# TensorE issues the score matmuls of four row strips one behind another in the pass for the exponentials

## What is computed

```python
qkv = x @ w_qkv                                    # x: 4096 tokens as 32 blocks of 128
scores = einsum('bhqd,bhkd->bhqk', q, k) / sqrt(8) # per sequence of 256 tokens, 16 heads
scores = where(causal, scores, finfo.min)
attn = softmax(scores, -1)
o = einsum('bhqk,bhkd->bhqd', attn, v) ... @ w_o
h = layernorm(x + o, g1, b1)
# then a mixture of 8 experts, 2 chosen per token, F = 512, and a second layernorm
```

## Time and profile before

| | us |
|---|---|
| median of 3 runs | 1197.24 |
| lowest and highest | 1195.87 and 1200.68 |
| profiled execution, first to last instruction (span) | 1192.8 |
| PE busy in it | 1022.4 (86%) |
| PE weight loads | 818.6 (69%) |
| DVE, ACT, POOL busy | 680.8, 670.5, 572.7 |

### The profile page before, as it was taken

How to read it: one execution, slowest core, us unless ns; L and a number is a source line. 1 busy time by engine, 2 the same in 40 slices (tenths; PEclk the granted TensorE clock), 3 DMA queues, 4 the chain that set the end, 5 groups by cost and what they waited for, 6 DMA issues and landing times. The chain is left out here.

```text
span 1192.8 us, 29724 instructions
## 1 busy us (share of the span) xinstructions
PE 1022.4 (86%) x10913; PEld 818.6 (69%) x10913; DVE 680.8 (57%) x2458; ACT 670.5 (56%) x1494; POOL 572.7 (48%) x693
## 2 busy tenths in 40 slices
PE   4799979998989989999989989998999988866470
PEld 2566656886877867686777867687777866766470
DVE  5657665655558835686568835686556723520314
ACT  1243424875758756675667757576666756534240
POOL 2223356235465455555565455554464456542515
PEclk9988877998999989898999979799999979887795
DMA  3394105555555545555556545555556545676562
GB/s 71 86 193 109 37 19 162 167 164 181 154 160 150 172 138 156 147 154 172 149 154 171 165 137 144 153 158 154 160 163 176 170 137 164 202 244 221 212 194 51
DMA packets 117239, 181.01 MB, mean 152 GB/s; under 512 B 13128, under 2 KB 80232, under 8 KB 117096
## 3 DMA queue, kind: packets, MB, share of 16 engines
q1 hardware_dynamic: 108904, 162.32, 47.7%
q0 software_dynamic: 8192, 16.79, 4.9%
HBM read 145.10 MB, written 38.68 MB: 154 GB/s over the span
## 5 line engine op out<-in xcount | busy, mean ns | idle before, releaser
L1173 POOL TENSOR_SCALAR_AFFINE_SELECT probs<-probs 128x512 f32<-128x512 f32 x256 | 182.5, 721 | 262.1 <-ACT probs L706 257.1
L706 ACT ACTIVATE probs<-ps_quad 128x768 f32<-128x768 f32 x256 | 193.7, 807 | 150.3 <-PE ps_quad L527 87.8
L744 ACT ACTIVATE act<-ps_ring,weights 128x128 f32<-128x128 f32 x696 | 191.8, 387 | 96.4 <-PE ps_ring L623 48.0
L874 DVE TENSOR_REDUCE shift_cols<-ps_quad 128x2 f32<-128x512 f32 (+3 forms) x256 | 149.9, 586 | 139.8 <-PE ps_quad L508 125.6
L632 PE MATMUL ps_ring<-weights,act 128*128 128x128 f32 x1392 | 190.8, 285 | 31.1 <-issue 16.4
L632 PEld LDWEIGHTS ps_ring<-weights,act 128*128 128x128 f32 x1392 | 174.5, 198 | 35.1 <-issue 21.6
L623 PE MATMUL ps_ring<-tile_t,weights 128*128 128x128 f32 x1392 | 187.6, 292 | 3.9 <-issue 3.2
L623 PEld LDWEIGHTS ps_ring<-tile_t,weights 128*128 128x128 f32 x1392 | 174.0, 204 | 16.8 <-issue 13.2
L1236 POOL DMA_INDIRECT picked<-sorted_outputs,place x128 | 123.7, 966 | 79.8 <-issue 78.6
L999 DVE TENSOR_TENSOR tile_y<-ps_ring,weights 128x128 f32<-128x128 f32 x174 | 48.8, 287 | 182.2 <-PE ps_ring L632 101.2
L1222 POOL DMA_INDIRECT sorted_rows<-h_rows,place x128 | 124.5, 972 | 53.5 <-issue 34.6
(11 more groups left out here) (165 smaller groups left out, 1531.5 us busy)
## 6 DMA issues: line engine op xcount, KB each, us to landing
weights<-expert_weights SPq DMA_DIRECT2D x174, 578.0 KB
tile_rows<-sorted_rows SPq DMA_DIRECT2D x56, 192.0 KB
sorted_outputs<-tile_y SPq DMA_DIRECT2D x56, 192.0 KB
query_key_parts<-qk SPq DMA_DIRECT2D x32, 256.0 KB, 5.0
k<-query_key_parts SPq DMA_DIRECT2D x64, 64.0 KB
q<-query_key_parts SPq DMA_DIRECT2D x64, 64.0 KB
sorted_rows<-zeros SPq DMA_DIRECT2D x2, 1472.0 KB, 10.7
xs<-in_L_attn_x SPq DMA_DIRECT2D x32, 64.0 KB, 2.3
```

Of the source, the lines that this page charges most:

```text
L706: sc.activation(probs[:, r % PROBS, 2 * a:2 * a + 2, :], ps_quad[:, 2 * a:2 * a + 2, 0:3 * P], ACT.Exp, scale=HD ** -0.5).then_inc(pair_fr ...
L744: ins = sc.activation(act[:, k % ACTS, f, :], bank(use)[:, f * P:(f + 1) * P], ACT.Gelu_apprx_tanh, bias=weights_of(k)[:, 2 * F + f:2 * F ...
L874: dve.tensor_reduce(shift_cols[:, late, groups], ps_quad[:, groups, 0:split], AX.X, ALU.max)
L1173: pool.affine_select(out=both, in_=both, compare_op=ALU.is_ge, fill=0.0, base=0, pattern=[[0, 2], [0, 2], [1, P]], channel_multiplier=-1). ...
```

## The change

In `exps` on PE the loop over pairs is split. PE first waits for both pairs to be free. Then it issues L523 for the strips 0 to 3, then L527 for the strips 0 to 3; `pair_full[0]` is signalled by the L527 of strip 1 and `pair_full[1]` by that of strip 3. Nothing else is changed: the same matmuls run on the same operands, `scores` stays as it was, and so do ACT, DVE, POOL and all DMAs. (Lines of PE behind `exps` move down by one.)

```diff
                 for a in range(2):
                     pe.wait_ge(pair_free[a], QUAD_NO["exps", n, j])
-                    for i in (2 * a, 2 * a + 1):
-                        rows = slice(32 * i, 32 * i + SLOT)
-                        pe.matmul(ps_quad[:, i, 0:P], k4[rows, par, j, at + P:at + S], q4s[rows, n % 2, j, P:S],
-                                  start=True, stop=True, tile_position=(32 * i, 0))
-                    for i in (2 * a, 2 * a + 1):
-                        rows = slice(32 * i, 32 * i + SLOT)
-                        mm = pe.matmul(ps_quad[:, i, P:3 * P], k4[rows, par, j, at:at + P], q4s[rows, n % 2, j, :],
-                                       start=True, stop=True, tile_position=(32 * i, 0))
-                    mm.then_inc(pair_full[a], 1)
+                for i in range(4):
+                    rows = slice(32 * i, 32 * i + SLOT)
+                    pe.matmul(ps_quad[:, i, 0:P], k4[rows, par, j, at + P:at + S], q4s[rows, n % 2, j, P:S],
+                              start=True, stop=True, tile_position=(32 * i, 0))
+                for i in range(4):
+                    rows = slice(32 * i, 32 * i + SLOT)
+                    mm = pe.matmul(ps_quad[:, i, P:3 * P], k4[rows, par, j, at:at + P], q4s[rows, n % 2, j, :],
+                                   start=True, stop=True, tile_position=(32 * i, 0))
+                    if i % 2:
+                        mm.then_inc(pair_full[i // 2], 1)
```

## The result

The changed kernel takes 1231.22 us (median of 4 runs, 1222.29 to 1238.12), the kernel before 1198.44 us (4 runs, 1195.87 to 1200.68). The ratio is 1.0263, with an interval of 1.0203 to 1.0322: about 33 us slower. The forecast was 1206 us, and at most 1214.

A forecast was written before the change was run, and what follows sets the result against it. PE's in-order list, with its few waits, was taken to set the pace. Late pair 0 cost 12.9 us, other terms 0; 30% absorbed left +9.0 us on 1197.2, so 1206 us, range 1197 to 1214.

The forecast's parts named there:

- rival B: In `exps` on PE, pairs run one after the other, so packing four strips gains 30 us: 1168 us; chance 0.05.
- step 2: PE's exit from waiting `exps` pieces: still 0.85 us after pair 1 is free, so cost 0.
- step 7: PE's other waits, such as "issue", absorb 30% of the 12.9 us delay, leaving +9.0 us.
- L: Theory formed after the result: the loss comes from ACT getting pair 0 of `exps` late, costing more than 9 us.
- step 4: Late pair 0 delays PE's next `scores` in 31 of 70 waiting pieces, 12.9 us; 39 pieces hide it.
- Step 1: Matmuls and loads of `exps`: none added or removed, cost 0, bounds -2 to +3 us.
- The check in the prediction: Sign to look for: PE's time from the last start to the exit of `exps` stays 0.85 to 0.88 us.
- Steps 3 and 4: ACT gets pair 0 of `exps` late, up to 0.73 us; PE feels it in 31 pieces, 12.9 us together.
- Step 6: ACT's copies and GELUs queued behind `exps` run late: 0 to 5 us, taken as 0.
- Rival A: PE's "issue" waits absorb 60 to 90% of the delay, no change: 1198 to 1202 us; chance 0.26.
- W: Theory formed after the result: waiting for both pairs has its own price on PE, paid in each waiting `exps` piece.

The follow-up runs named there:

- E4: Kernel before plus one wait, always already met, ahead of pair 1's own wait in `exps`; order and signals as before: 1209.88 us, ratio 1.0088.
- E3: Kernel before, PE's order and waits untouched, but pair 0 is signalled to ACT only by pair 1's matmuls: 1219.6 us, ratio 1.0164.
- E2: Kernel before with both waits ahead of the matmuls in `exps`, which still run pair by pair: 1227.01 us, ratio 1.0230.
- E1: Changed kernel with its two waits in the other order, pair 1's first: 1223.56 us, ratio 1.0190 to the kernel before.
- E9: Kernel before with pair 0's signal late only in the 31 `exps` pieces the prediction charged: 1069.06 us, ratio 1.0166.
- E10: Kernel before with pair 0's signal late only in the 39 `exps` pieces the prediction called hidden: 1054.92 us, ratio 1.0018.
- E5: The changed kernel once more, as it is, on another chip: 1221.59 us, ratio 1.0300 to the kernel before.
- E8: Kernel before with pair 0's mask matmuls L508, in the maxima pass, moved ahead of pair 1: 1190.08 us, ratio 1.0051.
- E6: Kernel before with the change, waits swapped, only in 58 `exps` pieces picked as having free banks: 1194.02 us, ratio 1.0072.
- E12: Kernel before with both waits ahead in the 58 pieces picked as free, matmuls still pair by pair: 1058.08 us, ratio 1.0057.

## Why the prediction was wrong

The direction was right, and so was the first reading: four strips are in flight already, there is nothing to pack (rival B), and what the change does is to hold pair 0 back. The size was wrong by a factor of over three and a half, 9 us for 33, and the steps that failed can be named. Of the 24 us that the forecast missed, step 2 is some 10 (E4), step 7 is 3.9, and L is 7 us larger than the 12.9 of step 4 (E3).

- **Step 1** (matmuls and loads cost nothing) holds. The order of the strips costs nothing that shows: E2 without it is as slow as the change. A free piece has its next load 0.881 us after its first before and 0.868 us after, at the median, within this step's bounds.
- **Step 2 failed.** It took PE's time from "pair 1 is free" to the exit as the same, 0.85 us, and the price of waiting as nothing. It is 0.06 us more to the first load and 0.04 us more to the exit, 0.105 us in each of some 70 pieces. Of the 43 ns at the exit some 13 come from pair 0 running beside pair 1 (E1's exit is 867 ns, for 854 before) and 30 from the wait that stands alone. Together that is 7.4 us; E4 measures 0.9%, 10 us, for the wait alone. The section on the change has the row that shows it: `[waits pair_free1,pair_free0]` on one matmul, where each had one wait before. The check in the prediction ("0.85 to 0.88 us") caught it: the exit is 0.897.
- **Steps 3 and 4 hold in place and are somewhat small.** E9 and E10 split the 70 pieces where step 4 does, and the one costs 1.7%, the other 0.2% with zero inside its interval. The steps of 0.67 and 0.22 us are measured as 0.675 and 0.23. The sum was 12.9; it is 14.4 between those two runs, and 17 us (12.6 to 22.2) for E9 against the kernel before. On the first chip, with the 39 other pieces late too, E3 gives 20 us (15 to 24). Where the 7 us above 12.9 arise isn't shown.
- **Step 6** (other work of ACT, 0 to 5 us) is E10's 0.2%, 2 us with an interval from -1.6 to +5.4. Taking 0 was fair.
- **Step 7 failed.** It let PE's waits for "issue" take up 30% of the delay, with 9.0 us left. They took up none that shows: the late signals cost at least 14.9 us in E3 and 12.6 in E9 by their intervals. In the rows of PE's matmuls, "issue" adds up to 44.7 us in 69 places before and 55.4 us in 79 after, and to 55 and 56.9 us in E3 and E4; these waits rather grow with the delay, though that is one trace of each. On the third chip, where such waits nearly vanish, L costs as much (E9, 1.7%). Rival A is out.
- **The granted clock**, which no step had, may make up some of the rest. In the first four runs its mean is 0.885 after and 0.896 before. From run to run of the same kernel the time goes by about 3.5 us for each 0.01 of granted clock, so the lower clock goes with about 4 us. That is a correlation over the runs (r = -0.57), and no run here sets the clock by itself; a slower run and a lower clock may both come from the gaps in PE's work. L and W don't need it: E3 and E4 are slower at a mean clock of 0.897, where the kernel before has 0.896 beside them.

Put together, L is 1.6% and W 0.9%, against 2.6% measured (3.0% in E5). The forecast had a smaller L, less 30% of it, and no W.

Rival B was taken from the Trainium skill (TensorE: Matmul & The Clock Gate, Part 3), by which matmuls keep program order in start and in end. For the starts the traces disagree: the second pair's matmuls start 27 ns behind the first's, ahead of the L527 that stand before them in the program, and E2, which differs from the change only in that order, takes the same time within the intervals. Of the ends they say nothing, since the profile models the ends of matmuls. What E8 adds is that this overtaking has a limit.

Left open: the 0.6 to 0.7% of E6 and E12. A wait met long before has no price within the piece, but what sets off the few large delays wasn't found. Leaving out the waits altogether was not tried, since pair 0's reader would then race with PE.

## What to carry to other kernels

A buffer handed on in halves is worth its early half: before tying the halves together, look in the timeline for who starts on the first half, and who waits for it next. Where a change puts two waits ahead of one instruction, look at which becomes an instruction of its own, and write first the one that is met last. And don't discount a delay on the engine that sets the pace because it has idle time elsewhere: show first that this idle time doesn't move with it.

## What was not expected of the hardware

- **A wait that stands alone and is met late** costs 62 ns to the first load and some 30 ns to the exit, against the same wait attached to the matmul: 115 and 883 ns in E4 for 53 and 854 before, and 115 and 897 ns in the change for 53 and 867 with its waits swapped (E1). The profile books it often as "issue" (69 places for L525 in E4, for 45 of L523 before).
- **How far TensorE lets matmuls of other row strips overtake.** With 16 records of loads and matmuls of another pair ahead, the second pair starts after 27 ns; with 20, four of them of the bf16 mask matmuls, after 0.25 us or more (E8). Whether it is their number that counts was not tested.
- **The same kernel takes 1199.6, 1184.3 and 1051.8 us on three chips.** On the third, PE's matmuls hardly wait for "issue". This is the only such row of them in E10, where the trace of the kernel before has 44.7 us in 69 places:

```profile
PE ps_ring L633 <- issue: 2.9, 3, 1.5
```

  E10's mean granted clock in this trace is 0.945, for 0.898 in that of the kernel before. The cause was not tested. The change was measured where the kernel before takes 1198.4 us and where it takes 1184.3 us (E5), and the ratios of 1.0263 and 1.0300 agree within their intervals. Neither it nor an edit of E1 to E8 was run on the third chip, so that ratios carry over to it isn't shown.
